# The end of a two-stage graph network: three phases over all nodes, and a pipeline by groups of seven node tiles

## The reference

```
    h = jax.nn.silu(h @ W2 + b2)
    messages = h @ W3 + b3
    aggregated = jax.ops.segment_sum(messages, dst, num_segments=N)
    update_input = jnp.concatenate([node_feats, aggregated], axis=-1)
    gate = jax.nn.sigmoid(update_input @ G + gb)
    u = jax.nn.silu(_layernorm(update_input @ U1 + ub1, ln1_g, ln1_b))
    update = _layernorm(u @ U2 + ub2, ln2_g, ln2_b)
    return node_feats + gate * update
```

## Time and profile before

| what | value |
|---|---|
| median of 3 runs | 3615.21 us (3613.82 to 3622.81) |
| the profiled execution: its time | 3614.43 us |
| its span | 3612.2 us |
| granted TensorE clock, mean of the span | 0.837 |
| busy share PE, PEld, DVE, ACT, POOL | 82%, 58%, 45%, 38%, 44% |

### The profile page before, as it was taken

One profiled execution on the slowest core, in us unless ns is written; L12 is line 12 of the kernel. 1 busy time (PEld: TensorE's weight loads), 2 busy tenths in 40 slices (PEclk: granted clock), 3 DMA queues, 4 the chain that ended last, 5 costly groups with the idle time before them and its releaser, 6 DMA issues.

```text
span 3612.2 us, 59613 instructions
## 1 busy us (share of the span) xinstructions
PE 2970.1 (82%) x17152; PEld 2102.1 (58%) x17152; DVE 1628.9 (45%) x3492; ACT 1389.0 (38%) x2083; POOL 1591.1 (44%) x1667
## 2 busy tenths in 40 slices
PE   3799999985986985788888898888888888888855
PEld 2577777765986985444554555445455454555455
DVE  7999999985015017322222222222222222222227
ACT  2788888872001001233333333333333333333312
POOL 4000000000000000777777777777777777777642
PEclk7899999997996995788878778888878888787756
DMA  3122222234973961466666666666666666666510
GB/s 115 72 124 107 124 107 124 107 148 190 395 320 139 395 264 57 118 165 164 163 163 166 164 161 167 168 164 162 166 163 166 164 166 164 164 164 165 140 35 18
DMA packets 352485, 576.87 MB, mean 160 GB/s; under 512 B 41884, under 2 KB 248862, under 8 KB 333384
## 3 DMA queue, kind: packets, MB, share of 16 engines
q1 hardware_dynamic: 299480, 467.64, 38.6%
q0 software_dynamic: 52976, 108.89, 14.0%
HBM read 388.48 MB, written 187.88 MB: 160 GB/s over the span
## 4 chain that ended last, share of the span: by engine, by line
POOL 31%; PE 24%; issue 18%; DVE 17%; DMA 7%; DVEq 2%; ACT 1%; POOLq 1%; ACTq 0%; SPq 0%
POOL arena L541 29%; PE ps L665 11%; DVE arena L1330 9%; DMA arena<-p_tab,m_idx 6%; PE ps L742 4%; PE ps L584 3%; PE ps L751 2%; PE ps L739 2%; PE ps L572 1%; DVEq L1330 1%; POOL ends L509 1%; PE ps L759 1%; DVE arena L1317 1%; DVE ybuf L1202 1%; DVE ends L1023 1%
## 5 line engine op out<-in xcount | busy, mean ns | idle before, releaser
L541 POOL DMA_INDIRECT arena<-p_tab,m_idx x1568 | 1486.5, 948 | 1864.6 <-issue 1832.3
L1406 DVE TENSOR_TENSOR_SCAN arena<-arena,ps 128x512 f32<-128x512 f32 x392 | 501.6, 1280 | 1036.5 <-ACT ps L922 937.8
L742 PEld LDWEIGHTS ps<-ident,arena 128*128 128x128 f32 x3136 | 488.0, 237 | 623.2 <-DMA arena<-p_tab,m_idx 463.9
L742 PE MATMUL ps<-ident,arena 128*128 128x128 f32 x3136 | 579.6, 342 | 278.6 <-DMA arena<-p_tab,m_idx 278.6
L917 ACT ACTIVATE arena<-ps 128x512 f32<-128x512 f32 x392 | 234.0, 597 | 1030.1 <-PE ps L742 1017.2
L665 PE MATMUL ps<-arena 128*128 128x192 bf16 (+1 forms) x5635 | 505.6, 248 | 66.7 <-DVE arena L1275 65.8
L751 PE MATMUL ps<-arena,weights 128*128 128x512 f32 x784 | 540.5, 782 | 0.0
L665 PEld LDWEIGHTS ps<-arena 128*128 128x128 f16 x5635 | 481.8, 98 | 81.1 <-issue 66.1
L1330 DVE TENSOR_SCALAR arena<-iota_w,arena 128x392 bf16<-128x392 f16 x2156 | 519.5, 314 | 0.0
L682 PE MATMUL ps<-arena 128*128 128x392 bf16 x2352 | 452.1, 336 | 70.9 <-DVE arena L1330 70.6
L739 PE MATMUL ps<-arena,weights 17*128 17x512 f32 x784 | 487.7, 704 | 0.0
(11 more groups left out here) (187 smaller groups left out, 1675.8 us busy)
## 6 DMA issues: line engine op xcount, KB each, us to landing
arena<-count_d SPq DMA_DIRECT2D x66, 1568.0 KB, 8.2
arena<-keep_d SPq DMA_DIRECT2D x392, 256.0 KB, 4.5
scan_rows<-arena SPq DMA_DIRECT2D x392, 256.0 KB
count_d<-arena SPq DMA_DIRECT2D x49, 1568.0 KB, 5.2
wide<-count_d SPq DMA_DIRECT2D x32, 1568.0 KB, 8.4
arena<-p_tab,m_idx POOLq DMA_INDIRECT x1568
arena<-attr_in SPq DMA_DIRECT2D x392, 34.0 KB
p_tab<-wide SPq DMA_DIRECT2D x7, 448.0 KB, 3.0
```

The lines of the kernel that those rows point to most:

```text
L541: pool.indirect_dma_start(m_rows[:, k, t, :], None, p_tab, bass.IndirectOffsetOnAxis(ap=m_idx[:, k, t:t + 1].bitcast(U32), axis=0))\
L742: last = pe.matmul(x[:, t * P:(t + 1) * P], m_rows[:, k, t, :], ident[:, :], start=False, stop=(t == TB - 1), skip_group_check=True)
L1406: dve.tensor_tensor_scan(m_scan[:, k % SCAN_RING, :], m_mask[:, k, :], m_term[k % TERM_RING], before, ALU.mult, ALU.add).then_inc(e1.scan_ ...
```

## The change

The three phases are replaced by one software pipeline over the groups; the rounds g = 0 to 7 hold group g's first half and group g-1's second half.

- W3 is folded into the update's weights. PE computes W3 @ UGa once (UGa: the rows of U1 and G that belong to the sums, side by side, 192 columns) and b3 @ UGa as a row, kept in `w_fold` and added to `UGx`. The pipeline multiplies the raw sums by `w_fold`.
- The biases ub1, gb, b3 and ub2 become rows of weights. h turned stays in `hT` from the table phase with two rows more, the node's degree and 1 (`deg_one`). So U1 and G are now two products each: one by `hT` (66 rows), one by the turned sums (128 rows), both summed in PSUM. U2 is a product of 128 rows and one of 2 rows.
- A node without edges now fetches a row of zeros (`scan_rows` has one row more, which SP stores at the start), so `has` is not multiplied.
- The squares of both norms move from DVE to ACT. DVE stages u straight out of PSUM. The Sigmoid is done for groups 0-1, 2-3, 4-5 and 6 after rounds 1, 3, 5 and 6 (`GATES_AT`).
- POOL's three operations at the end go; gain, bias and gate are applied by DVE by groups (`finish`), and each group's result is stored by its own DMA.
- Semaphores are merged: `alone` (one instead of five), `gathered`, `mask_loaded` and `stored` of a path that these inputs don't take.

```diff
+GATES_AT = {1: (0, 2), 3: (2, 4), 5: (4, 6), 6: (6, 7)}
...
-            sp.wait_ge(y_ready, 1)
-            sp.dma_start(out, xres[:, :, :]).then_inc(y_stored, DMA)
-            sp.wait_ge(y_stored, DMA)
+            for g in range(NG):
+                sp.wait_ge(y_ready, g + 1)
+                sp.dma_start(out[:, g * GT:(g + 1) * GT, :], xres[:, g * GT:(g + 1) * GT, :]).then_inc(y_stored, DMA)
+            sp.wait_ge(y_stored, NG * DMA)
...
-            node_phase(G_SUM, HID, [(W("W3"), D)])
-            node_phase(G_UPDATE, 2 * D, [(W("U1"), HID), (W("G"), D)], slots=1)
-            node_phase(G_OUT, HID, [(W("U2"), D)])
+            pe.transpose(ps[0:D, 0, 0:P], W("W3"), ident[:, :]).then_inc(w3_turned, 1)
+            pe.wait_ge(w3_copied, 1)
+            pe.matmul(ps[:, 2, 0:HID + D], w3T, W("UGa"), start=True, stop=True)
+            pe.matmul(ps[0:D + 2, 4, 0:HID + D], W("b3"), W("UGa"), start=True, stop=True).then_inc(folded, 1)
+            def turn_ends(g):
+                pe.wait_ge(e1.ends_ready, g + 1)
+                if g >= 1:
+                    pe.wait_ge(turned_kept, max(1, 2 * (g - 1)))
+                for t in range(GT):
+                    last = pe.transpose(ps[:, t // TB, (t % TB) * P:(t % TB + 1) * P], ends[:, g * GT + t, :], ident[:, :])
+                last.then_inc(turned, 1)
+            def update_in(g):
+                pe.wait_ge(turned_kept, max(1, 2 * g))
+                if g == 0:
+                    pe.wait_ge(fold_kept, 2)
+                if g >= 1:
+                    pe.wait_ge(gate_kept, g)
+                if g >= 2:
+                    pe.wait_ge(u_staged, g - 1)
+                for t in range(GT):
+                    at = (g * GT + t) * P
+                    u = ps[:, 2 + 2 * (g % 2) + t // TB, (t % TB) * HID:(t % TB + 1) * HID]
+                    gate = ps[:, 6, t * D:(t + 1) * D]
+                    of_ends = turned_rows[0][:, t * P:(t + 1) * P]
+                    pe.matmul(u, hT[:, at:at + P], W("UGx")[:, 0:HID], start=True, stop=False, skip_group_check=True)
+                    pe.matmul(gate, hT[:, at:at + P], W("UGx")[:, HID:], start=True, stop=False, skip_group_check=True)
+                    pe.matmul(u, of_ends, w_fold[:, 0:HID], start=False, stop=True, skip_group_check=True)
+                    last = pe.matmul(gate, of_ends, w_fold[:, HID:], start=False, stop=True, skip_group_check=True)
+                last.then_inc(u_done, 1)
+            def turn_hidden(g):
+                pe.wait_ge(u_staged, g + 1)
+                pe.wait_ge(turned_kept, 2 * (g + 1) if g + 1 < NG else 2 * g + 1)
+                for t in range(GT):
+                    last = pe.transpose(ps[:, t // TB, (t % TB) * P:(t % TB + 1) * P], stage[:, g % 2, t, :], ident[:, :])
+                last.then_inc(turned, 1)
+            def update_out(g):
+                pe.wait_ge(turned_kept, 2 * g + 3 if g + 1 < NG else 2 * NG)
+                if g >= 1:
+                    pe.wait_ge(v_squared, g)
+                for t in range(GT):
+                    at = (g * GT + t) * P
+                    v = ps[:, 7, t * D:(t + 1) * D]
+                    pe.matmul(v, turned_rows[1][:, t * P:(t + 1) * P], W("U2"), start=True, stop=False, skip_group_check=True)
+                    last = pe.matmul(v, hT[D:D + 2, at:at + P], W("ub2")[D:D + 2, :], start=False, stop=True, skip_group_check=True)
+                last.then_inc(v_done, 1)
+            for g in range(NG + 1):
+                if g < NG:
+                    turn_ends(g)
+                    update_in(g)
+                if g >= 1:
+                    turn_hidden(g - 1)
+                    update_out(g - 1)
...
-            node_phase(G_SUM, HID)
-            node_phase(G_UPDATE, 2 * D)
-            sqrt(NORM_U)
-            act.wait_ge(gate_in, 1)
-            act.activation(ybuf[:, :, :], ybuf[:, :, :], ACT.Sigmoid).then_inc(gate_done, 1)
-            node_phase(G_OUT, HID, func=ACT.Silu, scale=W("ln1_g"), bias=W("ln1_b"))
-            sqrt(NORM_O)
+            act.wait_ge(w3_turned, 1)
+            act.activation(w3T, ps[0:D, 0, 0:P], ACT.Copy).then_inc(w3_copied, 1)
+            def banks(b):
+                return ps[:, b:b + 2, :].rearrange("p b c -> p (b c)")[:, 0:GC]
+            def keep_turned(g):
+                act.wait_ge(turned, max(1, 2 * g))
+                if g >= 1:
+                    act.wait_ge(u_done, g)
+                act.activation(turned_rows[0], banks(0), ACT.Copy).then_inc(turned_kept, 1)
+            def square_u(g):
+                act.wait_ge(u_done, g + 1)
+                if g >= 1:
+                    act.wait_ge(u_reduced, g)
+                act.activation(u_squares.rearrange("p t c -> p (t c)"), banks(2 + 2 * (g % 2)), ACT.Square).then_inc(u_squared, 1)
+            def hidden_silu(g):
+                act.wait_ge(turned, 2 * g + 3 if g + 1 < NG else 2 * NG)
+                if g >= 1:
+                    act.wait_ge(v_done, g)
+                act.activation(turned_rows[1], banks(0), ACT.Silu, scale=W("ln1_g"), bias=W("ln1_b")).then_inc(turned_kept, 1)
+            def keep_v(g):
+                act.wait_ge(v_done, g + 1)
+                v = ps[:, 7, 0:GT * D]
+                if g >= 2:
+                    act.wait_ge(y_ready, g - 1)
+                act.activation(v_rows[g % 2].rearrange("p t c -> p (t c)"), v, ACT.Copy).then_inc(v_kept, 1)
+                if g >= 1:
+                    act.wait_ge(v_reduced, g)
+                act.activation(v_squares.rearrange("p t c -> p (t c)"), v, ACT.Square).then_inc(v_squared, 1)
+            def gates(g0, g1):
+                act.wait_ge(gate_kept, g1)
+                part = ybuf[:, g0 * GT:g1 * GT, :]
+                act.activation(part, part, ACT.Sigmoid).then_inc(gate_done, 1)
+            for g in range(NG + 1):
+                if g < NG:
+                    keep_turned(g)
+                    square_u(g)
+                if g >= 1:
+                    hidden_silu(g - 1)
+                    keep_v(g - 1)
+                act.wait_ge(var_ready, NORM_END + g)
+                new, old = (0 if g < NG else GT), (2 * GT if g >= 1 else GT)
+                act.activation(rstd[:, new:old], var[:, new:old], ACT.Sqrt).then_inc(sd_ready, 1)
+                if g in GATES_AT:
+                    gates(*GATES_AT[g])
...
                 dve.wait_ge(start_summed, 1)
                 dve.tensor_copy(start_f[:, :], ps[:, 2, 0:J]).then_inc(starts_read, 1)
                 dve.wait_ge(starts_read, 1)
                 link(dve.tensor_tensor(degree[:, :], end_f[:, :], start_f[:, :], ALU.subtract))
                 link(dve.tensor_scalar(has[:, :], degree[:, :], 1.0, None, ALU.min))
+                last_edges(link)
+            def last_edges(link):
+                link(dve.tensor_copy(deg_one[:, :, 0], degree[:, :]))
+                link(dve.scalar_tensor_tensor(end_f[:, :], end_f[:, :], -1.0 - EPAD, has[:, :], ALU.add, ALU.mult))
+                link(dve.tensor_scalar(end_f[:, :], end_f[:, :], float(EPAD), None, ALU.add))
+                dve.tensor_copy(end_idx[:, :], end_f[:, :]).then_inc(ends_known, 1)
...
-                                                               per_node(rstd[:, bass.ds(g * GT, GT)], D), ALU.mult),
-                       lambda g, s: dve.tensor_tensor(group(wide, g), product(4 + 2 * s, HID), per_feature(V("b1"), GT), ALU.add))
+            def stage_h(g, s):
+                dve.tensor_tensor(stage[:, s, :, 0:D], group(ybuf, g), per_node(rstd[:, bass.ds(g * GT, GT)], D), ALU.mult)
+                return dve.tensor_copy(stage[:, s, :, D:D + 2], group(deg_one, g))
+            node_phase(G_TABLE, stage_h,
+                       lambda g, s: dve.tensor_tensor(group(ends, g), product(4 + 2 * s, HID), per_feature(V("b1"), GT), ALU.add))
             link(dve.tensor_copy(m_idx[:, :, :].rearrange("p k t -> p (k t)"), src_all[:, 0:LOOP * TB]))
...
-            inverse_deviation(link, NORM_O, D)
-            scale_by_rstd(link, upd, D)
-            dve.wait_ge(gate_scaled, 3)
-            link(dve.tensor_tensor(upd, upd, ybuf[:, :, :], ALU.mult))
-            dve.tensor_tensor(xres[:, :, :], upd, hbuf[:, :, :], ALU.add).then_inc(y_ready, 1)
+            dve.wait_ge(folded, 1)
+            dve.tensor_copy(w_fold, ps[:, 2, 0:HID + D]).then_inc(fold_kept, 1)
+            dve.tensor_tensor(W("UGx"), W("UGx"), ps[0:D + 2, 4, 0:HID + D], ALU.add).then_inc(fold_kept, 1)
+            link = Chain(chain["end"])
+            def keep_gate(g):
+                dve.wait_ge(u_done, g + 1)
+                dve.tensor_copy(ybuf[:, g * GT:(g + 1) * GT, :], ps[:, 6, 0:GT * D].rearrange("p (t c) -> p t c", t=GT))\
+                   .then_inc(gate_kept, 1)
+            def deviations(g):
+                if g < NG:
+                    dve.wait_ge(u_squared, g + 1)
+                    dve.tensor_reduce(var[:, 0:GT], u_squares, AX.X, ALU.add).then_inc(u_reduced, 1)
+                if g >= 1:
```

(34 more changed lines are left out.)

161 lines of the change are left out of this document (81 added, 80 removed).

## The result

The changed kernel took 3658.76 us (median of four runs, 3639.40 to 3678.79) where the kernel before took 3616.55 (3613.82 to 3622.81, four runs): 1.0115 of it, 95% interval 1.0058 to 1.0171. It is slower, as forecast, by 42 us where I had said 28, and 3 us above the top of my range. The run that was profiled is its fastest: 3639.40 us with a span of 3637.3.

The account below looks back on a forecast made before the run. The prediction attacked the tail's serial phases after the fetches; PE's instructions at 1.2 GHz and ACT's chain would bind the new rounds. Tail +27.8 and the rest +1.0 on 3614.43 gave 3643 us, range 3616 to 3656.

Parts of the forecast that it names:

- The last copy of turned rows: ACT's copy in the tail; a start before 3580 would show that ACT's order does not bind.
- The folding of W3: Between the last scan and the first group, some 4 us of work expected to cost nothing there.
- the short set: PE's 28 product instructions per group for v, bias included; 6.08 us at 0.217 us apiece.
- One round: Chain of PE and ACT steps for one group in the tail; 25.9 us, or 28.1 with gates.
- the end of the last group: Steps after round 6's Sqrt with nothing beside them, from 3619.6 to 3636.7, before the output transfer.
- the rival of cheap bias rows: Two-row bias products in the tail cost almost nothing: 21 us less, 3622 us; chance 0.06.
- The front: Everything before the new tail, expected to change by +1.0 us in small DVE and table-phase additions.
- 1.2 GHz in the tail: TensorE's clock taken as 1.2 GHz, granted 0.50, throughout the new pipeline.
- rival (2): Clock rises in each round's long product set and falls in the pause behind it: 3617 us; chance 0.11.
- long sets: PE's 56 product instructions per group for U1 and G in the tail; 12.15 us each.
- (b) and (c): Old tail after the fetches: remaining W3, update and second layer, then three DVE passes and one output; 119.8 us.
- (a): Old tail's first part: POOL's 49 fetches of last rows, one group about every 8.7 us, beside W3 only.

Follow-up runs that it names:

- apart: Changed kernel with each group's seven 128-row last products first and the seven two-row bias products behind them; 4233.90 us, 1.0142 of the kernel before.
- order66: Changed kernel with the last bias taken over 66 rows and the pipeline's steps reordered; 3599.81 us, 0.9951 of the kernel before.
- after_third: The changed kernel run again, unedited; 3653.18 us, 1.0118 of the kernel before.
- wide66: Changed kernel with the 66-row bias, old order, and one 192-column product in place of 128 and 64; 3612.17 us, 0.9992 of the kernel before.
- order_only: Changed kernel with the reordered steps alone, keeping the two-row bias; 3603.06 us, 1.0001 of the kernel before.
- both66: Changed kernel with the 66-row bias, the reordered steps and the 192-column products; 3562.39 us, 0.9854 of the kernel before.

## Why the prediction was right in sign and too low

**The mechanism held.** Copies, tables, waits and their order are as written, and the round is bound by PE's instructions with ACT's steps between them. Table loads: 19 in eight rounds, one in the first and two or three in each of the others. The last copy of turned rows starts at 3587.9, after 3580. The fetched rows of the last group wait some 100 us for PE; I had 90. The folding of W3 lies before the first group, as said, and the last-edge result comes 0.2 us later (809.78 for 809.62), where I had 0.5.

**The term that was mis-sized is the 28 instructions of the short set**, 6.08 us in "One round" and in the end of the last group. They took 8.71 in five rounds of seven and 8.08 and 7.95 in two where the clock rose for a while: 17.0 us more in all. I took the price from the earlier trace rows, where all 28 instructions have 128 rows, and wrote that I count instructions. The row that bore on it stood in the earlier trace rows: a load of 17 rows took 0.145 us where one of 128 rows took 0.121. I used it only against the rival of cheap bias rows, and not as a bound on the dear side; by it a bias instruction is no cheaper, and may be dearer by a fifth or more. The experiments put the excess where those two rows hinted: few-row weights in turn with full ones. The Trainium skill, page "TensorE: Matmul & The Clock Gate", section "LDWEIGHTS (loading the stationary operand)", which I cited as agreeing, has the time of a weight load go with columns and not rows. apart agrees with it (two-row products in sequence take 0.227 us each), the alternation does not (0.308), and the measurement decides. Why few rows in turn with many are dear, no trace here shows.

**What came out shorter.** A round without the short set is 27.7 - 8.7 = 19.0 us where I had 19.8: hand-overs, a Sqrt of 0.21 and a copy of 0.90. Over the rounds and the end that is 6 us back. First group to end: 200.1 us forecast (3439.9 to 3640.0), 210.8 measured (3426.5 to 3637.3), +10.7 = 17.0 - 6.3.

**The front was forecast as if it stood still.** I gave it +1.0 us and no width. It moves by steps. At one and the same moment, the same instructions of a layer's product phase (windows, before and then after; columns as in the earlier trace rows):

```profile
1090.00:1108.00 18.00, 17.52 (x84) 17.34 (x83) 10.59 (x19) 4.03 (x4) 0.00 (x0) 0.50 0.04 18
```

```profile
1090.00:1108.00 18.00, 7.92 (x69) 7.56 (x68) 15.92 (x22) 5.51 (x6) 0.00 (x0) 0.83 0.05 19
```

In both traces this phase's first turning starts at 1076.51 and the code is the same; the clock is granted at 1.2 GHz throughout in one and rises in the other, which ends the phase 8 us sooner. Two such phases make the 17 us between 594 and 612, and the first deviations themselves come at 836 to 837 or at 849 to 864. Why the clock rises in one run and not in another is not shown. Over the ten traces with the shorter message stage the last scan starts between 3406.7 and 3450.9 us. The changed kernel's four runs span 39 us for this reason, I take it, since its tail was 226.7 and 225.3 in two traces; before's own runs beside order66 span 40 us. With a tail of 226.7, the front of before's profile gives 3652.8 us, inside my range, and that of after_third 3658.3, outside. The range held the pipeline's unknowns and left out the front's.

**The clock.** 1.2 GHz in the tail was right for this kernel, but for short rises, and rival (2) was wrong here: in the profile of after all seven long sets ran at 0.50, and the clock rose only behind two of them, from 3545.7 to 3549.1 and from 3573.0 to 3576.4. In after_third one long set caught such a rise and took 11.12 us. The clock was at 1.00 in five of seven long sets of wide66 (192 columns for 128 and 64) and in three of order66. The Trainium skill's rule that sustained activity releases the slow state (same page, section "What's actually happening") agrees with those sets, and not with the long sets of the changed kernel, busy without a break at 0.50, nor with those of order_only.

**What it cost to be a pipeline.** The change puts (b) and (c) beside (a), but with 84 product instructions a group at 1.2 GHz, and with PE waiting for ACT twice a round, 31.4 us in all. Both are repairable: with the other order, the 66-row bias and the wide products the same idea is 51 us shorter than before's tail, and both66 is 1.5% faster than before, about 2.6% faster than the changed kernel by the two ratios.

## What to carry to other kernels

When phases over everything become a pipeline by groups, write the order so that TensorE always has a product set between handing rows to another engine and needing them back; here the order alone gave back 32.5 of the 37 us that the change lost. Give a small extra product more rows, filled with zeros (here 66 beside neighbours of 128), or group the small ones: a two-row product between full ones made each instruction cost almost half as much again. Compare such versions by the stretch that they change: nineteen runs of the unedited kernel before span 40 us on one chip, as much as the whole change costs.

## What the runs showed of the hardware that I had not expected

- fp32 instructions of 64 columns at 1.2 GHz: 0.213 us each in turn with 66 rows from partition 0, 0.227 for either kind in sequence, 0.308 with two rows in turn with 128, whether the two begin at partition 64 or 0.
- The granted clock was 0.50 through 11.00 busy us of 11.00 in a long set of order_only, and 0.95 over 5.80 busy us of 5.80 in a long set of order66. The two kernels differ only in their bias products, with 2 rows and with 66. There is one trace of each.
- The clock of an identical phase, begun at the same 0.01 us, was 0.50 in one run and 0.83 in another.
- On two of the four chips of the experiments the messages took 2483 to 2525 us against 1963 to 1967, and in the four traces of the changed end there ACT went on 36 to 42 us after PE had ended its first long set, 8.3 to 8.7 us after the last fetch was issued.
